# A fused patch-embedding, attention and expert kernel: last group image by image, first patches from transposed rows, later patches over 128 partitions

## The reference

```python
patches = patchify(x, 16)                       # (32, 36, 768)
h = concat([cls, patches @ W.T + b], 1) + pos   # (32, 37, 256)
h = concat([h, txt], 1)                         # (32, 114, 256)
n = layernorm(h)
h = h + n + causal_attention(n, Wq, Wk, Wv, 16 heads of 64) @ Wo
n = layernorm(h)
gates = softmax(n @ router_w + router_b)        # 8 experts, top 2, capacity 570
h = h + sum_e gate_e * (gelu(n @ w1[e] + b1[e]) @ w2[e] + b2[e])   # for the tokens that e holds
```

## Time and profile before

| | us |
|---|---|
| median of 3 runs (887.63 to 888.59) | 888.34 |
| the profiled execution | 888.15 |
| its span in the trace | 886.40 |
| PE busy | 841.6 (95%) |
| DVE, ACT, POOL busy | 563.8, 508.7, 375.0 |
| first `scores` of the loop starts at | 45.40 |
| last output projection (image 3) starts at | 624.34 |
| expert phase's first weights products after | 654.51 |

### The profile page before, as it was taken

How to read it: one execution, slowest core, us unless ns; L and a number is a source line. 1 busy time by engine, 2 the same in 40 slices (tenths; PEclk the granted TensorE clock), 3 DMA queues, 4 the chain that set the end, 5 groups by cost and what they waited for, 6 DMA issues and landing times.

```text
span 886.4 us, 20329 instructions
## 1 busy us (share of the span) xinstructions
PE 841.6 (95%) x7103; PEld 763.1 (86%) x7103; DVE 563.8 (64%) x2458; ACT 508.7 (57%) x1688; POOL 375.0 (42%) x678
## 2 busy tenths in 40 slices
PE   6799999999999999999999999999579999999996
PEld 6688898888889889888888988988569999999995
DVE  3567438566674855866576486477557877668771
ACT  3477657556674765666467377566055555556551
POOL 2144334254543724544364373465614223441334
PEclk9999999999999999999999999999779999999999
DMA  8333120011003102101200110010446444543322
GB/s 237 100 101 153 44 56 23 2 52 49 24 14 78 33 1 68 44 13 36 60 18 2 38 30 6 9 33 3 122 127 194 110 128 115 126 134 96 69 27 28
DMA packets 55575, 57.69 MB, mean 65 GB/s; under 512 B 26831, under 2 KB 47579, under 8 KB 55360
## 3 DMA queue, kind: packets, MB, share of 16 engines
q1 hardware_dynamic: 34834, 45.15, 16.4%
q0 software_dynamic: 18944, 9.76, 6.9%
q10 hardware_dynamic: 1696, 1.49, 0.6%
HBM read 34.25 MB, written 21.89 MB: 63 GB/s over the span
## 4 chain that ended last, share of the span: by engine, by line
PE 80%; DVE 11%; issue 3%; SPq 2%; DMA 1%; ACT 1%; POOL 1%; POOLq 0%; DVEq 0%
PE bank L409 14%; PE bank L411 14%; PE bank L410 14%; PE o_bank L1324 5%; PE score_bank L1304 5%; PE pT_bank L1313 5%; PE bank L1192 3%; DVE sm L1021 2%; PE o_bank L410 2%; PE o_bank L411 2%; PE o_bank L409 2%; PE score_bank L409 2%; PE score_bank L410 2%; PE score_bank L411 2%; PE bank L1274 1%
## 5 line engine op out<-in xcount | busy, mean ns | idle before, releaser
L598 POOL TENSOR_SCALAR pr<-pr,rc 114x114 f32<-114x114 f32 x512 | 181.0, 370 | 300.9 <-DVE rc L1063 299.8
L740 ACT ACTIVATE pr<-sm,nb 114x114 f32<-114x114 f32 x512 | 192.3, 383 | 7.8 <-DVE nb L1025 7.6
L629 POOL DMA_INDIRECT out_dram<-yout,dest x40 | 74.1, 1852 | 159.9 <-ACT yout L786 158.4
L1021 DVE CUSTOM_DVE_ANT_0 sm<-score_bank,mask 114x114 f32<-114x114 f32 x512 | 109.9, 272 | 49.8 <-PE score_bank L1304 49.7
L409 PE MATMUL bank<-xT_hi,wqkv_hi 128*128 128x456 f32 (+1 forms) x288 | 110.8, 385 | 3.0 <-ACT vv L649 1.7
L734 ACT ACTIVATE pT<-pT_bank 114x456 f32<-114x456 f32 x128 | 70.5, 551 | 53.3 <-PE pT_bank L1313 52.8
L410 PE MATMUL bank<-xT_lo,wqkv_hi 128*128 128x456 f32 (+1 forms) x288 | 100.2, 348 | 0.0
L411 PE MATMUL bank<-xT_hi,wqkv_lo 128*128 128x456 f32 (+1 forms) x288 | 100.1, 348 | 0.0
L740 ACT ACTIVATION_READ_ACCUMULATOR pr<-sm,nb 114x1 f32 x512 | 99.0, 193 | 0.0
L713 ACT ACTIVATE oT_hi<-o_bank 128x228 fp32r<-128x228 f32 x128 | 45.3, 354 | 79.2 <-PE o_bank L1324 69.1
L1313 PE MATMUL pT_bank<-ident,pr 114*114 114x114 f32 x512 | 74.3, 267 | 0.7 <-ACT pT L734 0.7
(11 more groups left out here) (203 smaller groups left out, 2254.7 us busy)
## 6 DMA issues: line engine op xcount, KB each, us to landing
stage_a<-in_L_ffn_w_dram SPq DMA_DIRECT2D x8, 1024.0 KB
stage_b<-in_L_ffn_w_dram SPq DMA_DIRECT2D x8, 1024.0 KB
slots_dram<-fill SPq DMA_DIRECT2D x8, 605.6 KB
pix<-in_x_dram SPq DMA_DIRECT2D x96, 36.0 KB, 2.2
xs<-slots_dram SPq DMA_DIRECT2D x8, 363.4 KB
hraw<-in_txt_dram SPq DMA_DIRECT2D x8, 308.0 KB
out_dram<-h SPq DMA_DIRECT2D x8, 308.0 KB
xs<-slots_dram SPq DMA_DIRECT2D x8, 242.2 KB
```

Source lines behind the costliest of these rows:

```text
L598: p = pool.tensor_scalar(pr[:, m % 4, i, :], pr[:, m % 4, i, :], rc[:, m % 4, i:i + 1], 1.0, ALU.mult, ALU.mult)
L629: pool.indirect_dma_start(out, bass.IndirectOffsetOnAxis(ap=dest[e % 2][:, t:t + 1], axis=0), yout[:, t, :], None, compute_op=ALU.add).the ...
L740: a = act.activation(pr[:, N % 4, i, :], sm[:, N % 2, i, :], ACT.Exp, bias=nb[:, N % 2, i:i + 1], scale=SCALE, accum_out=rs[:, N % 4, i:i ...
L1021: m = dve.tensor_tensor_reduce(sm[:, N % 2, i, :], score_bank[i % 2][0:T, o:o + T], mask[:, :], 1.0, NEG, ALU.add, ALU.max, mx[:, N % 2, i ...
```

## The change

**Prologue.** Groups 0 and 1 are embedded in another way (`load_first`, `pack_first`, `transpose_first`, `embed_first`): one transfer brings the group's pixels as 72 rows (image, channel, patch row) of 6 KB, ACT and DVE reorder them, PE transposes them (12 transposes), and 12 matmuls with a contraction of 128 follow, against weights `first_W` in a matching order. The other groups use weights `embW`, transposed again from a reordered copy (`tok_turned`), 12 more transposes. Wv is issued by ACT once the patch weights have arrived, Wk and Wq by SP once Wv has arrived, and all three are split in halves of columns in the order of need. Wo is split in the loop at step 2. The class token comes from a zero column in `embT` and a row of `base`, in place of a transfer. `stay_warm` goes from 16 and 16 to 6.

**Later groups.** A half group's pixels are loaded by 8 transfers, each to 16 partitions and shifted by 2 pixels more than the one before (`load_pixels`): 16 transfers a group, straight from HBM. ACT packs them in two halves (steps 5 and 11) and `embed` runs 12 matmuls with a contraction of 128.

**Last group.** Q and K are projected for all four images at once, in 16 jobs at steps -3 to 1 (`LAST_QK`), and kept (`last_qk`). A step covers four heads of one image (`heads_of`), so an image is finished every four steps. Image b is output-projected at steps 10, 13 and 17 of the group, image 3 after the loop; `Y` and `L` of the first unit stand at steps 16 and 17 (`LAST_Y`, `LAST_L`), the sending of group 6 at steps 15 to 17 (`LAST_DISPATCH`).

```diff
-PR = CH * PX
-HPX = PX // 2
+SH, JJ = 8, 2
+JS = CH * JJ
+FIRST = GB * CH * NPS
+PIX = GB // 2 * CH * NPS * IMG
...
-        AT_PACK, AT_RSTD1, AT_RSTD2 = 4, 10, 8
+        AT_PACK, AT_RSTD1, AT_RSTD2 = [(2, 11)] + [(5, 11)] * (G - 1), 10, 8
+        AT_WO = 2
...
-        ROUTE_LAST = [{14: (0,), 15: (1, 2)}, {12: (0,), 13: (1, 2), 14: (3, 4)}]
+        ROUTE_LAST = [{14: (0,), 15: (1, 2)}, {12: (1, 2), 13: (3, 4)}]
...
-        AT_HALF_O = 14
+        LAST_O, LAST_Y, LAST_L, LAST_C, ROUTED_C = {10: 0, 13: 1, 17: 2}, 16, 17, 14, 15
+        LAST_DISPATCH = {15: (0, 1), 16: (2, 3, 4), 17: (5, 6, 7)}
+        LAST_QK = {-3: ("K0",), -2: ("Q0", "K1", "Q1"), -1: ("K2", "Q2", "K3", "Q3"), 0: ("K4", "Q4", "K5", "Q5"), 1: ("K6", "Q6", "K7", "Q7")}
+        LAST_V = [{2: 0, 6: 1, 8: 2, 11: 3}, {3: 0, 7: 1, 9: 2, 12: 3}]
...
-            return (f, n // 2, 2 * (n % 2)) if f < LAST else (f, n % HP, 2 * (n // HP))
+            return (f, n // 2, 2 * (n % 2)) if f < LAST else (f, 2 * (n % (HP // 2)), n // (HP // 2))
...
+            def load_pixels(g, i):
+
+                if (g, i) == (2, 0):
+                    sp.wait_ge(filled, job_filled("P0", 3))
+                else:
+                    sp.wait_ge(packed, packed_units(g, i) - 1)
+                src = rows_of_images(GB * g + 2 * i)
+                for h in range(SH):
+                    dst = pix[PX * h:PX * (h + 1), :].rearrange("r (n w) -> r n w", w=IMG)
+                    sp.dma_start(dst[:, :, 0:IMG - JJ * h], src[:, :, JJ * h:IMG]).then_inc(pix_in, 16)
...
+            load_first(0)
             sp.dma_start(tok_raw[:, :, :], tokW.rearrange("(c p) f -> p c f", p=128)).then_inc(tokW_in, 16)
-            load_pixels(0)
...
+            sp.wait_ge(wv_in, 16)
+            sp.dma_start(stage_c[:, :].rearrange("p (c n) -> p c n", c=KC), Wk.rearrange("(c p) n -> p c n", p=128)).then_inc(wk_in, 16)
             sp.dma_start(stage_b[:, :].rearrange("p (c n) -> p c n", c=KC), Wq.rearrange("(c p) n -> p c n", p=128)).then_inc(wq_in, 16)
...
-                    for j in range(HPX):
-                        m = pe.matmul(dst[:, k * GB * NP:(k + 1) * GB * NP], embW[:, j, k * 128:(k + 1) * 128], tok[:, j, :],
-                                      start=(j == 0), stop=(j == HPX - 1))
+                    for j in range(JS):
+                        m = pe.matmul(dst[:, k * GB * NP:(k + 1) * GB * NP], embW[:, j, k * 128:(k + 1) * 128], tok[:, j % JJ, :, j // JJ, :],
+                                      start=(j == 0), stop=(j == JS - 1))
...
-                if N == STEPS + 2:
+                if N == AT_WO + 1:
+                    dve.wait_ge(wo_hi_done, 1)
+                    split_low(wo_lo[:, :, :], stage_d[:, :].rearrange("p (c n) -> p c n", c=HP), wo_hi[:, :, :], wo_lo_done)
+                if k == LAST_L + 1:
+                    route(FIRST_HALF, 1)
+                if k - 1 in LAST_O:
+                    add_last(LAST_O[k - 1])
+                if k == ROUTED_C - 1:
+                    last_moments(FIRST_HALF)
+                if k == ROUTED_C:
                     for b in unit_images(FIRST_HALF):
                         normalise_rows(FIRST_HALF, b)
+                if k == LAST_L + 1:
+                    route(FIRST_HALF, 2)
```

618 lines of the change are left out of this document (364 added, 254 removed).

## The result

The changed kernel takes 895.69 us (median of 4 runs, 894.6 to 897.43), the kernel before 888.0 on the same chip: ratio 1.0087, 95% interval 1.0074 to 1.01. It is slower by 7.7 us, where 879.7 was forecast, 8.6 faster. The profiled execution took 894.6 with a span of 892.6, 6.2 more than before.

The account below looks back on a forecast made before the run. PE's own work was taken to bound the kernel (busy 95% of the span), except where PE runs dry. Terms -5.8 - 2.0 - 5.2 + 2.0 + 4.9 - 2.5 = -8.6 from 888.15 gave 879.6 us; 8-in-10 range 871.5 to 885.

Parts of the forecast that it names:

- The Wo term: Loop's first group: Wo split at step 2 makes ACT late for the transposed probabilities; +2.0 us, bounds 0 and +4.
- rival 3: Loop: pixel transfers, issued by pieces, set the pace and ACT stands in its pack; 927 us, chance 0.05.
- The last group's idle term: Last group: PE, its work moved forward, waits for DVE late in the group; +4.9 us, bounds 0 and +8.
- The clock: Prologue: PE's clock falls after idle gaps with fewer `stay_warm`; +1.0 us, counted within the prologue's term.
- Behind the last O: After the last output projection: less routing ahead of normalising (-1.1), group 6 sent earlier (-1.4); -2.5 us, bounds -4 and +1.
- The prologue: Before the loop: X starts near 20.5, loop at 40.2 instead of 45.40; -5.2 us, bounds -8 and 0.
- the embedding at three quarters: Groups 2 to 7: 12 embedding instructions instead of 16, -0.96 us a group; -5.8 us, bounds 0 and -7.7.
- the traffic beside PE without cost in the steady groups: Loop groups: a half group's 4608 pieces need 7.7 us, within 27.5 us allowed, so transfers do not set the pace.
- Wk and Wq not in the way: Prologue: denies rival 2, where chained weight loads leave the prologue no gain; 884.1 us, chance 0.18.
- Q and K at full width: Last group: 16 jobs of 6 matmuls over 456 columns, 20.7 against 22.7 us; -2.0 us, bounds -2.6 and +1.

Follow-up runs that it names:

- run 5: Changed kernel with the pack of group 2's first half of pixels at step 5 and the last group as in the kernel before: 882.46 us, ratio 0.9921.
- run 3: Changed kernel with only DVE's order in the last group moved, two routing parts placed later: 893.68 us, ratio 1.0045.
- Run 9: Changed kernel with output projections of the last group's images 0 and 1 at steps 14 and 15, followers one or two steps later: 891.88 us, ratio 1.0038.
- run 11: Changed kernel with 11 matmuls of the identity put into each of PE's two long waits of the tail: 892.83 us, ratio 1.0049.
- runs 6 and 7: Changed kernel with 20 identity matmuls in each of the tail's two waits: 894.48 us; the same plus pack at step 5 and DVE's later routing: 888.54 us.
- runs 5 and 10: The second: changed kernel with the pack at step 5 and output projections of the last group's images 0 and 1 at steps 14 and 15: 884.15 us.
- run 8: Changed kernel without half of the shifted pixel copies, pack over 64 partitions, result not the reference's: 890.13 us, ratio 1.0019.
- run 12: Changed kernel with pack at step 5, old last group, and ACT's half of the Wo split moved before the loop: 882.56 us, ratio 0.9929.
- run 13: Changed kernel with pack at step 5, late output projections of images 0 and 1, and 4 identity matmuls before the last projection: 884.43 us.

## Why the prediction was wrong

By its own terms, in the cuts of the first section (forecast, then measured against the kernel before):

```
loop's first scores                       -5.2    -4.2
first group (Wo term)                     +2.0    +9.9
embeddings up to M7                       -4.8    -5.2
last group and all behind it              -0.6    +5.7
sum                                       -8.6    +6.2
```

(-0.6 is -1.0 of group 7's embedding, -2.0 of keys and queries, +4.9 of idle time, -2.5 behind the last O. +5.7 is 4.60 up to the last scores, 1.36 to the last scatter, -0.23 in the rest.)

**The Wo term failed, in the note behind it.** "The first pixels of group 2, issued about 34 and landed by about 46 at the latest, are needed at 48" rested on 27 ns a packet, by which 4608 packets take 7.8 us where I left 12. The transfer needed 69 ns a packet, was issued at 36.88 and landed at 55.08. The rows behind the 27 ns were of unshifted pieces; the shifted ones come at 307 in a us for all engines, and seven eighths of 4608 at that pace are 13 us. I used the packet price only for rival 3, at the steady pace of a group, where it indeed does not bite (27.5 us allowed, about 18 used), and never asked for the one place where the same transfer has 14 us (36.88 to the pack's turn at 50.57). Without the wait the term is +2.9 (run 5) against +2.0. The rule that the prediction weighed there, of the Trainium skill (DMA: Bandwidth & Descriptors, Specifications), pointed the right way: pieces under 512 B moved 1.74 MB in 16 us here, 109 GB/s with the engines' share at 129%, and I let the row outvote it. It has no price, though, and pieces of 384 B, also under its bound, took 22 ns at the median in both kernels.

**The last group's idle term was in the right place and lacked the main part.** Forecast were waits for DVE's `oT_lo`, and they are there, 2.79 and 2.75. Their repair (run 3) takes 1.0 from each and gives 2.5 us with the clock that comes back. What I missed is that two output projections were moved ahead of the last scores. PE was full there, so each microsecond put before the last scores delays the chain that starts with them: scores, masks, exponentials, scaling, transposes, outputs, the last projection, norm, routing, scatters. I counted the moved work as neutral since PE does it anyway. Run 9, with nothing but their places and their followers' changed, gives 5.7 us back ahead of the last scores and loses 0.6 behind. In the old order these projections fill PE's waits in the last steps.

**The clock** stands in the prologue's term and was left out of the tail, where the forecast itself had 6.5 us of idle time. Filling the two waits gives 2.9 us back (run 11).

**Behind the last O**: forecast -2.5. From the start of that projection to the experts' transposes it is 29.2 us against 30.2 before, -1.0; the projection itself took 4.4 us instead of 2.9, at the low clock. Where it ran at full clock, from its start to the last scatter it is 18.8 us in runs 6 and 7, 19.2 in run 3 and 20.0 in run 11, against 21.3 before: -2.5, -2.1 and -1.3. So most of this step's miss is the clock. The gain of 1.4 from sending group 6 early was real too: the last unit's scatters no longer queue, they wait for their slots.

**The prologue** came out 1.0 short, by a premise that failed: "the patch weights arrive as now (PE starts at 5.83)". In the changed kernel the group's pixels are issued ahead of them, and PE starts at 8.11:

```profile
8.11 2.79 PE L1502 MATMUL bank<-ident,tok_raw 128*128 128x128 f32 x12 [8.11 <-DMA tok_raw<-in_L_tok_W_dram]
```

X then starts at 23.75 instead of the 20.5 of the forecast; from V to the loop PE took less than I had counted. No run moved the weights ahead.

**Right**: the embedding at three quarters (3.12 us where the earlier trace rows has 4.10; from M2 to M7 -5.2 against -4.8), the traffic beside PE without cost in the steady groups, Wk and Wq not in the way. **Half right**: Q and K at full width. A job takes 1.24 us and PE works 1.6 us less, but waits of 1.4 us come with it (runs 5 and 10), which the forecast had only in its bound of +1. The prologue's -5.2 is -4.2 in this trace and -2.8 over the seventeen traces of changed kernels (a loop start of 42.6 on average, against the one trace of before), so its middle was too good.

## What to carry to other kernels

When work is moved on a full engine, ask what stands behind it: moved ahead of the last item that starts a long chain, it cost its whole length here, however full the engine looked. Price a transfer by its packets where its slack is smallest, not at the steady pace, and take the price from pieces that start and end as the new ones do, not from pieces of like size. A thin end pays for the wait, and for the clock that falls in it. Where two chains meet in it (here the last unit's slots and the row of scatters), look in the trace which of them the last consumer waited for, and look again after each edit: an edit that shortens one can lengthen the other, and then the time says nothing about either.

## What the runs showed of the chip

- Packets of 384 B, whole rows of the input, took 22 ns at the median in the kernel before and in the unshifted copy of the changed one, there at 678 in a us with the 16 engines' share at 100%. Packets of 376 to 328 B, rows from 8 to 56 B on, took 68 to 73 at 307 in a us; in run 8 it was 22 and 74 to 75. So it is not their number, nor how many are under way. Whether it is the start within the row, the gap that it leaves in the destination, or standing behind the first copy, no run tells.
- GpSimd and VectorE held each other up in run 12. VectorE's subtraction for `wo_lo` takes 2.29 us in the kernel before; here it took 3.18, and GpSimd's `hx` ran in its first 1.0. Of the eight scalings behind, the first took 2.40 us, until the subtraction was over, and the other seven 0.36 each:

```profile
51.87 3.18 DVE L915 TENSOR_TENSOR wo_lo<-stage_d,wo_hi 128x2048 fp32r<-128x2048 f32 x1
```

```profile
51.64 1.27 POOL L677 TENSOR_TENSOR hx<-hraw,xn 114x512 f32<-114x512 f32 x1
52.89 4.80 POOL L668 TENSOR_SCALAR pr<-pr,rc 114x114 f32<-114x114 f32 x8
57.99 1.40 POOL L668 TENSOR_SCALAR pr<-pr,rc 114x114 f32<-114x114 f32 x4 [0.31 <-DVE rc L1205]
```

  The Trainium skill (GPSIMD Engine Reference, Specifications) says that GpSimd shares its SBUF interfaces with VectorE, and that instructions of VectorE with two SBUF inputs contend; this subtraction has two, and the rows agree.
- POOL paused 3.6 to 5.3 us from its third scatter to its fourth in each trace looked at (616.50 to 620.05 in run 13, 616.57 to 621.91 in run 5). Where it waited for nothing and had nothing else in between, it sent one each 1.43. No run looked for the reason.
